# Four buffers instead of two for the selective scan, and two-column-block weight loads for the experts, in a four-layer kernel

## The chip, the cores and the metric

The kernel runs on the 8 cores of one Trainium2 chip. Each core gets one of the 8 sequences of the batch (2048 tokens of 1024 features) and a copy of all weights, and works through the whole four-layer model alone. There is no traffic between cores.
The metric is the device time of the slowest core in microseconds. Engines are named as in the profile: PE is TensorE, DVE is VectorE, ACT is ScalarE, POOL is GpSimd.

## The reference

Each layer is `x = x + s * g`, where `s` is a sequence mixer and `g` a SiLU of a feed-forward part, both taken from the layer-normed `x`. What matters for this change is the selective scan of layer 0 and the experts and the attention of layer 2:

```python
# layer 0, mixer: d_inner = 2048 channels, 16 states, 2048 steps
dA = jnp.exp(dt_i[..., None] * A)
h  = dA * h + dt_i[..., None] * B_i[:, None, :] * x_i[..., None]
y  = jnp.einsum('bds,bs->bd', h, C_i)
...
# layer 2, feed-forward: 8 experts, each takes its k best tokens
k = int(EXPERT_CAPACITY * t / e)
g, m = jax.lax.top_k(probs.transpose(0, 2, 1), k)
h = jax.nn.gelu(jnp.einsum('nekd,edf->nekf', x[batch_idx, m], w1))   # 1024 -> 4096
h = jnp.einsum('nekf,efd->nekd', h, w2)                               # 4096 -> 1024
...
# layer 2, mixer: causal attention, 16 heads of 64, w_qkv and w_out
```

Here `k` is 512 tokens for each expert (2.0 * 2048 / 8).

## The kernel before, in words

Each engine has its own instruction list, written out in Python order, and five engines meet only through semaphores. The helper `emit` makes every instruction of an engine wait for the engine's own previous instruction too, so nothing of one engine overlaps with itself. `barrier` separates the four layers.

**Layer 0.** The 2048 tokens go in 8 slices of 256. In each slice the projections of `W_in`, a convolution, the low-rank feed-forward and the broadcast of B and C come first. Then the scan stage runs over 16 blocks `ct` of 128 channels. A block begins with `dt` (L635, L640, L642), and DVE's `dtx = dt * x` (L646). Then there are 16 steps `s`, one for each state. In each step

- ACT computes `exp(dt * A[s])` into one of two buffers `da2` (L655),
- POOL computes `u = dtx * B[s]` into one of two columns of `m8`, 7 or 6 (L659); an element there stands every 8 elements,
- DVE scans along the 256 tokens with both as inputs and writes column `s` of `Hbuf` (L664).

Because there are two buffers of each kind, ACT and POOL wait in step `s` for the scan of step `s-2`. After the 16 scans DVE alone does the block's end: it saves the last state (L670), multiplies by C (L672), adds the 16 states in a tree (L674 to L681), and applies D and the gate (L683, L687). The tree uses the columns of `m8` that held `u`. Then comes `dtx` of the next block, for which POOL waits.

**Layer 2.** For each of the 8 experts and each half `ic` of its tokens (256), a loop over `fc` goes through 32 blocks of 128 hidden columns. PE computes the hidden block of `fc` (8 matmuls of L270 into `pmisc` or `ptp`), ACT applies the Gelu (L1433), and PE then adds the product of the block `fc-1` with `w2` (8 matmuls, L1447). Weights stream through two buffers each: `w1_ld` fetches 128 columns of `w1`, `w2_ld` 128 rows of `w2`. All these DMAs are issued by POOL in order (L204), and each waits for PE to have used up what stood in its buffer. The attention behind it has a third stream `qkv_ld` with buffers of its own, and `w_out` comes through `w1_ld`.

Of the kernel before, what the change touches and what calls it, by code (L numbers as in the profile page):

```python
# [15 lines left out]
T = 2048  # L16
# [5 lines left out]
TS = 256  # L22
# [96 lines left out]
def build_program(active=(0, 1, 2, 3)):  # L119
# [7 lines left out]
    W = {}  # L127
# [42 lines left out]
    wbuf_t = sbt("wbuf", [128, 10240], BF16)  # L170
    pers_t = sbt("pers", [128, 8704], BF16)
# [27 lines left out]
    STA = F32Arena()  # L199
    WB = ColArena(wbuf_t, 10240)  # L200
# [142 lines left out]
    def make_stream(buf2):  # L343
        sems = (stream_sem_pool.pop(0), stream_sem_pool.pop(0))
        state = {"last": [0, 0]}

        def load(idx, dram_ap, reshape=None, rows=128):
            bufv = buf2[0:rows, idx % 2, :]
            if reshape:
                bufv = bufv.rearrange(reshape[0], **reshape[1])  # L350
            b.wait("gpsimd", "T", state["last"][idx % 2])
            return bufv, (sems[idx % 2],
                          dma("gpsimd", bufv, dram_ap, sems[idx % 2]))

        def consumed(idx, ttarget):
            state["last"][idx % 2] = ttarget
        return load, consumed

    def layer0():
# [60 lines left out]
        m8 = AR.alloc(TS * 8, "p (t s) -> p t s", t=TS)  # L420
# [9 lines left out]
        prod = ybuf[:, 0:8, :]  # L430
        xp_f = STA.alloc(TS)
        dt_f = STA.alloc(TS)
        da2 = [STA.alloc(TS), STA.alloc(TS)]
        cacc2 = [STA.alloc(TS), STA.alloc(TS)]

        b.emit("gpsimd", lambda e: e.memset(hstate[:, :, :], 0.0))
# [12 lines left out]
        for sl in range(NS2):  # L449
# [176 lines left out]
            scan_tgts = []  # L626
            dtx_tgt = 0
            for ct in range(16):
                bi = pbi[0] % POOLN[0]
                pbi[0] += 1  # L630
                bank = pb[bi]
                prev = evac_after_bank.get(bi)
                if prev is not None:
                    b.wait("tensor", prev[0], prev[1])
                b.emit("tensor", lambda e, ct=ct, p=bank: e.matmul(  # L635
                    p[:, 0:TS], wdt[0:64, ct, :], xp_bf[0:64, :],
                    start=True, stop=True), inc="T")
# [12 lines left out]
                for s in range(DS):  # L650
                    if len(scan_tgts) >= 2:
                        b.wait("scalar", "V", scan_tgts[-2])
                        b.wait("gpsimd", "V", scan_tgts[-2])
                    b.emit("scalar", lambda e, ct=ct, s=s, d=da2[s % 2]:
                           e.activation(out=d, in_=dt_f, func=AF.Exp,  # L655
                                        scale=a_sb[:, ct, s:s+1]), inc="S")
                    sS = b.cnt["S"]
                    gU = b.emit("gpsimd", lambda e, s=s, u=ub2[s % 2]:
                                e.tensor_mul(out=u, in0=dtx,  # L659
                                             in1=brep[:, s, :]), inc="G")  # L660
                    b.wait("vector", "S", sS)
                    b.wait("vector", "G", gU)
                    stg = b.emit("vector", lambda e, ct=ct, s=s, d=da2[s % 2],
                                 u=ub2[s % 2]: e.tensor_tensor_scan(  # L664
                                     out=Hbuf[:, :, s], data0=d,
                                     data1=u,
                                     initial=hstate[:, ct, s:s+1],
                                     op0=ALU.mult, op1=ALU.add), inc="V")
# [529 lines left out]
    def layer2():  # L1198
# [23 lines left out]
        cumf = pers_t[:, 4096:8192].bitcast(F32)  # L1222
        PT = pers_t[:, 0:8192].rearrange("p (tt i) -> p tt i", tt=16)
        cmask = pers_t[:, 8192:8320]
        w1_buf = WB.alloc(2 * 1024, "p (b2 m) -> p b2 m", b2=2)
        w2_buf = WB.alloc(2 * 1024, "p (b2 m) -> p b2 m", b2=2)
        XgT = WB.alloc(8 * 512, "p (k i) -> p k i", k=8)
        hT2 = [WB.alloc(256), WB.alloc(256)]
        pmisc2 = [pmisc[:, 0:256], ptp2[0].bitcast(F32)[:, 0:256]]
        gwsb = WB.alloc(1024)  # L1230
        gwT = WB.alloc(8 * 8, "p (k e) -> p k e", k=8)
        w1_ld, w1_done = make_stream(w1_buf)
        w2_ld, w2_done = make_stream(w2_buf)

# [25 lines left out]
            tp_state["evacs"].append(vv)  # L1260

        b.wait("tensor", "V", xnV)
        for tt in range(NTT):
            transpose_tiles([(xn[:, tt, dc*128:(dc+1)*128], xnT_tt[:, dc, :])
                             for dc in range(8)])
# [110 lines left out]
            evac_after_bank[bi] = ("V", tgt)  # L1376
        selV = b.cnt["V"]

        b.wait("vector", "V", selV)
        for ex in range(8):  # L1380
            for tt in range(NTT):
# [21 lines left out]
            for ic in range(2):  # L1403
                hgel = {}
                w2bs = {}
                for fc in range(33):
                    if fc <= 31:
                        w1b, t1 = w1_ld(ex*64 + ic*32 + fc,
                                        W["l2_w1"][ex][:, fc*128:(fc+1)*128]
                                        .rearrange("(k p) m -> p k m", p=128),  # L1410
                                        ("p (k m) -> p k m", dict(k=8)))
                        w2b, t2 = w2_ld(ex*64 + ic*32 + fc,
                                        W["l2_w2"][ex][fc*128:(fc+1)*128, :])
                        w2bs[fc] = (w2b, t2)
# [8 lines left out]
                        def evh(e, p, par=fc % 2):  # L1423
# [4 lines left out]
                                  for kt in range(8)], 128, 256, None,  # L1428
# [5 lines left out]
                                              out=hT2[par],  # L1434
                                              in_=pmisc2[par][0:128, 0:256],
                                              func=AF.Gelu), inc="S")
                        w1_done(ex*64 + ic*32 + fc, b.cnt["T"])
                    fo = fc - 1
                    if 0 <= fo <= 31:
                        b.wait("tensor", "S", hgel[fo])  # L1440
# [67 lines left out]
        for dk in range(8):  # L1508
# [5 lines left out]
        xnT = xn.rearrange("p tt d -> p (tt d)").rearrange(  # L1514
            "p (k t) -> p k t", k=8)
        QK = wbuf_t[:, 0:2048]
        Kb = wbuf_t[:, 6816:8864]
        Vp2 = wbuf_t[:, 2048:3088].rearrange("p (kt w) -> p kt w", kt=16)
        wqkv_buf = wbuf_t[:, 3104:5152].rearrange("p (b2 m) -> p b2 m", b2=2)
        wtp_buf = wbuf_t[:, 5152:5664].rearrange("p (k m) -> p k m", k=8)  # L1520
        stage = wbuf_t[:, 5664:6688]
        at4 = pers_t[:, 8192:8704].rearrange("p (s t) -> p s t", s=4)
        cmask2 = wbuf_t[:, 6688:6816]
        ctxh = P_g.rearrange("p i t -> p (i t)").rearrange(
            "p (tt d) -> p tt d", tt=8)
# [668 lines left out]
```

How the kernel before makes its waits and increments, by code:

```python
    def emit(self, eng, fn, inc=None, n=1):  # L43
        esem = self.ESEM.get(eng)
        chain = esem is not None and inc in (None, esem)
        if chain:
            prev = self.cnt[esem]
            eh = self.semh[esem]
            if prev > 0:
                self.prog[eng].append(
                    lambda e, h=eh, v=prev: e.wait_ge(h, v))
            self.cnt[esem] += 1
            tgt = self.cnt[esem]
            def run(e, fn=fn, h=eh):
                fn(e).then_inc(h, 1)
            self.prog[eng].append(run)
            return tgt
        h = self.semh.get(inc)
        if inc is not None:
            self.cnt[inc] += n
        tgt = self.cnt.get(inc)
        def run(e, fn=fn, h=h, n=n, inc=inc):
            r = fn(e)
            if inc is not None:
                r.then_inc(h, n)
        self.prog[eng].append(run)
        return tgt
# [1 line left out]
    def wait(self, eng, sem, val):  # L71
        if val <= 0:
            return
        h = self.semh[sem]
        self.prog[eng].append(lambda e, h=h, v=val: e.wait_ge(h, v))
# [1 line left out]
    def barrier(self):  # L77
# [2 lines left out]
        h = self.semh["bar"]  # L80
        for eng in ENGS:
            es_ = self.ESEM.get(eng)
            if es_ is not None and self.cnt[es_] > 0:
                eh, ev = self.semh[es_], self.cnt[es_]
                self.prog[eng].append(lambda e, h2=eh, v=ev: e.wait_ge(h2, v))
            self.prog[eng].append(lambda e, h=h: e.sem_inc(h, 1))
            self.prog[eng].append(lambda e, h=h, v=tgt: e.wait_ge(h, v))
```

## Time and profile before

| | |
|---|---|
| time, median of 3 runs | 36100.56 us (36100.11 to 36105.73) |
| profiled execution, its own time | 36104.31 us |
| its span, slowest core (core 0) | 36102.3 us |
| spans of the 8 cores | 36067.7 to 36102.3 us |
| granted TensorE clock | 1.0 on every core |
| busy: PE, DVE, ACT, POOL | 47%, 25%, 18%, 14% |

The profiled execution lies 3.75 us above the median of the runs, and 2.0 us of its time lies outside the span. In a row of the profile the engine comes first or second, then the line of the kernel, the operation, what it writes and reads (by the names of the tensors, so that everything in the large work area is `arena`), the partitions and elements, and how many there are. Shares are of the span. No engine is busy over half of the time, so a share by itself tells little: the layers come one behind the other, and each has its own limit.

### The profile page before, as it was taken

To read this page: it belongs to the slowest core of one execution; us is meant where nothing else is said; L and a number is where in the kernel's file an instruction comes from. 1 tells how busy PE (TensorE), PEld (TensorE's weight loads), DVE (VectorE), ACT (ScalarE), POOL (GpSimd) and SP (SyncE) were. 2 spreads that over 40 slices of the span, in tenths; PEclk is the share of its full clock that TensorE was granted. 3 is DMA by queue.
4 is the path that set the end of the run, shared out by engine and by line. 5 is a ranking of instruction groups with operands and counts; after the bars stand their busy time and mean duration, and the time that the engine had idled before them with its cause. 6 is when DMAs were issued, how large, how long until landed. Compare 5 with 4: busy or idle time off the path is not lost.

```text
span 36102.3 us, 268160 instructions; the slowest of 8 cores (36067.7 to 36102.3 us)
## 1 busy us (share of the span) xinstructions
PE 16788.4 (47%) x51767; PEld 5456.9 (15%) x51816; DVE 9026.3 (25%) x17948; ACT 6637.6 (18%) x10746; POOL 5100.0 (14%) x4680
## 2 busy tenths in 40 slices
PE   2221122211555574666666655666444444444444
PEld 0000000000111121111111122222111111111111
DVE  4446644466212213111111111000100000012222
ACT  1111111111000000000000010111256656630000
POOL 3334433344110000111111000000000000000000
DMA  1111011110331011333333300000000000001112
GB/s 26 19 19 13 6 19 19 19 13 7 39 39 20 13 16 17 41 44 45 42 38 41 36 5 3 3 3 3 1 2 1 1 2 1 1 13 26 27 26 35
DMA packets 1385941, 671.96 MB, mean 19 GB/s; under 512 B 986448, under 2 KB 1254000, under 8 KB 1384544
## 3 DMA queue, kind: packets, MB, share of 16 engines
q0 software_dynamic: 1380256, 637.70, 15.4%
q1 hardware_dynamic: 4288, 17.11, 0.1%
q8 instruction: 697, 11.42, 0.1%
q14 instruction: 700, 5.73, 0.1%
HBM read 1283.30 MB, written 8.39 MB: 36 GB/s over the span
## 4 chain that ended last, share of the span: by engine, by line
PE 41%; issue 25%; DVE 15%; ACT 10%; POOL 5%; DMA 2%; DVEq 1%; ACTq 0%; POOLq 0%; another core or an unknown queue 0%; SPq 0%
PE pb L270 22%; DVE arena L664 6%; POOL arena L659 5%; PE pb L1447 4%; PE ptp L294 4%; ACT L1914 4%; PE pmisc L270 2%; PE ptp L270 2%; ACT arena L1917 2%; ACT stat L1914 2%; PE pb L1484 2%; ACT pers L1630 2%; PE pb L1622 1%; DVE arena L672 1%; PE pb L2071 1%
## 5 line engine op out<-in xcount | busy, mean ns | idle before, releaser
L270 PE MATMUL pb<-arena,wbuf 128*128 128x256 bf16 (+2 forms) x7616 | 3316.8, 436 | 3284.1 <-DVE arena L687 1857.5
L659 POOL TENSOR_TENSOR arena<-arena 128x256 bf16<-128x256 bf16 x2048 | 3268.9, 1596 | 2498.0 <-DVE arena L646 1627.6
L664 DVE TENSOR_TENSOR_SCAN arena<-stat,arena 128x256 bf16<-128x256 f32 x2048 | 3269.9, 1597 | 1146.3 <-POOL arena L659 1033.0
L270 PE MATMUL pb<-wbuf,arena 128*128 128x64 bf16 (+2 forms) x9888 | 2814.8, 285 | 1533.3 <-DVE wbuf L300 35.3
L1928 PE MATMUL pb<-arena 128*128 128x65 bf16 x4096 | 885.5, 216 | 2576.7 <-ACT arena L1917 2116.4
L655 ACT ACTIVATE stat<-stat,pers 128x256 f32<-128x256 f32 x2048 | 1040.4, 508 | 4377.7 <-DVE arena L664 4371.4
L635 PE MATMUL pb<-arena,pers 64*128 64x256 bf16 x128 | 47.1, 368 | 3806.8 <-ACT stat L642 3776.6
L1447 PE MATMUL pb<-wbuf 128*128 128x256 bf16 x4096 | 1515.6, 370 | 614.4 <-PE ptp L270 0.2
L294 PE MATMUL ptp<-cstb,wbuf 128*128 128x128 bf16 (+1 forms) x4480 | 1120.0, 250 | 1296.3 <-PE ptp L294 430.9
L270 PEld LDWEIGHTS pb<-arena,wbuf 128*128 128x128 bf16 (+1 forms) x7616 | 845.5, 111 | 5717.4 <-issue 5717.4
L204 POOL DMA_DIRECT2D wbuf<-L_ffn_w x1024 | 735.1, 722 | 5919.9 <-PE ptp L270 4092.4
L270 PEld LDWEIGHTS pb<-wbuf,arena 128*128 128x128 bf16 x9888 | 1036.8, 105 | 3312.4 <-issue 3312.4
L1914 ACT ACT_TABLE_LOAD x1023 | 1312.5, 1283 | 1217.8 <-PE pb L1908 1142.7
L300 DVE COPY wbuf<-ptp 128x128 bf16<-128x128 bf16 (+1 forms) x4480 | 967.6, 216 | 2006.4 <-PE ptp L294 1883.3
L1630 ACT ACTIVATE pers<-pb 128x128 bf16<-128x128 f32 x2176 | 602.8, 277 | 4031.0 <-PE pb L1622 3961.5
L1917 ACT ACT_TABLE_LOAD x1024 | 1313.8, 1283 | 79.7 <-ACT stat L1914 2.5
L1459 DVE CAST pers<-pb 128x256 bf16<-128x256 f32 x128 | 54.3, 425 | 4280.2 <-PE pb L1447 4268.4
L1939 DVE RECIPROCAL stat<-pb 128x4 f32<-128x4 f32 x64 | 11.7, 182 | 4242.0 <-PE pb L1928 4242.0
L1928 PEld LDWEIGHTS pb<-arena 128*128 128x128 bf16 x4096 | 429.1, 105 | 3363.6 <-issue 3363.6
L270 PE MATMUL pmisc<-wbuf 128*128 128x256 bf16 x2048 | 757.8, 370 | 323.0 <-DVE arena L300 9.1
L270 PE MATMUL ptp<-wbuf 128*128 128x256 bf16 x2048 | 757.8, 370 | 307.2
L204 POOL DMA_DIRECT2D wbuf<-L_ffn_W_v x144 | 75.7, 526 | 5737.9 <-PE pb L270 4743.7
(340 smaller groups left out, 16840.7 us busy)
## 6 DMA issues: line engine op xcount, KB each, us to landing
wbuf<-L_ffn_w POOLq DMA_DIRECT2D x1024, 256.0 KB, 4.7
wbuf<-L_attn_W_in POOLq DMA_DIRECT2D x128, 512.0 KB, 5.9
wbuf<-L_attn_W_out POOLq DMA_DIRECT2D x64, 512.0 KB, 6.8
wbuf<-L_ffn_We POOLq DMA_DIRECT2D x64, 512.0 KB, 5.4
wbuf<-L_ffn_W_k POOLq DMA_DIRECT2D x128, 256.0 KB, 3.9
wbuf<-L_ffn_W_r POOLq DMA_DIRECT2D x128, 256.0 KB, 3.9
wbuf<-L_ffn_W_v POOLq DMA_DIRECT2D x128, 256.0 KB, 3.9
wbuf<-L_ffn_V POOLq DMA_DIRECT2D x256, 64.0 KB, 2.5
```

The lines of the kernel that those rows point to most:

```text
L204: return b.emit(queue, lambda e, o=out_ap, i=in_ap, sk=slow_ok: e.dma_start(out=o, in_=i, allow_slow_non_contiguous=sk), inc=sem, n=16)
L270: r=out_rows, c=out_cols: e.matmul(p[0:r, 0:c], lh, rh, start=st_, stop=sp_),
L294: tT = b.emit("tensor", lambda e, s=s, a=srcp, idn=idn: e.transpose(ptp2[s][:, 0:idn], a, ident[0:idn, 0:idn]), inc="T")
L300: e.tensor_copy(out=d, in_=ptp2[s][:, 0:idn]),
L655: e.activation(out=d, in_=dt_f, func=AF.Exp, scale=a_sb[:, ct, s:s+1]), inc="S")
L659: e.tensor_mul(out=u, in0=dtx, in1=brep[:, s, :]), inc="G")
L664: u=ub2[s % 2]: e.tensor_tensor_scan(out=Hbuf[:, :, s], data0=d, data1=u, initial=hstate[:, ct, s:s+1], op0=ALU.mult, op1=ALU.add), inc="V")
L1447: coff=coff, w2b=w2b, par=fo % 2: e.matmul(bank[:, coff:coff+256], w2b[:, mt*128:(mt+1)*128], hT2[par], start=(fo == 0 and mt % 2 == 0), s ...
L1630: p=sbank: e.activation(out=at4[:, sl4, :], in_=p[:, 0:128], func=AF.Exp, scale=0.125),
L1914: e.activation(out=sd2[par], in_=p[:, 0:512], func=AF.Sqrt, bias=1e-12))
L1917: e.activation(out=ksq_at[:, par*512:par*512+512], in_=sd2[par % 2], func=AF.Exp, scale=-1.0), inc="S")
L1928: par=kav % 4, p=cbank: e.matmul(p[:, qm*65:qm*65+65], ksq_at[:, par*512+qm*128: par*512+(qm+1)*128], Vp3[:, kav, :], start=(kav == 0 and ...
```

## The change

There are four edits.

1. In the scan of layer 0 there are four buffers for `exp(dt * A)` and four columns of `m8` (7, 6, 5, 4) for `u`. ACT and POOL wait in step `s` for the scan of step `s-4`.
2. In the experts of layer 2, `w1` is fetched 256 columns at a time, for two values of `fc`, into two buffers of double size. To make room, the Gelu's output moves to `pers`, and the gate's weights lie in the first expert buffers. The first loads of `w1` and `w2` therefore wait for what reads the gate's weights.
3. The attention of layer 2 places its tiles elsewhere in `wbuf`, over memory of the experts that is free by then.
4. `w_out` and `w_qkv` of layer 2 both come through the stream of `w2`. `w_qkv` had its own before.

```diff
-        da2 = [STA.alloc(TS), STA.alloc(TS)]
+        da2 = [STA.alloc(TS), STA.alloc(TS), STA.alloc(TS), STA.alloc(TS)]
...
-                ub2 = [m8[:, :, 7], m8[:, :, 6]]
+                ub4 = [m8[:, :, 7], m8[:, :, 6], m8[:, :, 5], m8[:, :, 4]]
                 b.wait("gpsimd", "V", dtx_tgt)
                 for s in range(DS):
-                    if len(scan_tgts) >= 2:
-                        b.wait("scalar", "V", scan_tgts[-2])
-                        b.wait("gpsimd", "V", scan_tgts[-2])
+                    if len(scan_tgts) >= 4:
+                        b.wait("scalar", "V", scan_tgts[-4])
+                        b.wait("gpsimd", "V", scan_tgts[-4])
...
-        w1_buf = WB.alloc(2 * 1024, "p (b2 m) -> p b2 m", b2=2)
+        w1_buf = WB.alloc(2 * 2048, "p (b2 m) -> p b2 m", b2=2)
...
-        hT2 = [WB.alloc(256), WB.alloc(256)]
+        hT2 = [pers_t[:, 8192:8448], pers_t[:, 8448:8704]]
...
-        gwsb = WB.alloc(1024)
-        gwT = WB.alloc(8 * 8, "p (k e) -> p k e", k=8)
+        gwsb = w1_buf[:, 0, 0:1024]
+        gwT = w2_buf[:, 0, 0:64].rearrange("p (k e) -> p k e", k=8)
...
+        w1_done(0, b.cnt["T"]); w1_done(1, b.cnt["T"])
+        w2_done(0, b.cnt["T"]); w2_done(1, b.cnt["T"])
...
                     if fc <= 31:
-                        w1b, t1 = w1_ld(ex*64 + ic*32 + fc,
-                                        W["l2_w1"][ex][:, fc*128:(fc+1)*128]
+                        if fc % 2 == 0:
+                            w1b2, t1 = w1_ld(ex*32 + ic*16 + fc//2,
+                                             W["l2_w1"][ex][:, fc*128:(fc+2)*128]
...
+                        w1b = w1b2[:, :, (fc % 2)*128:(fc % 2)*128+128]
+                        t1 = t1_hold
...
-                        w1_done(ex*64 + ic*32 + fc, b.cnt["T"])
+                        if fc % 2 == 1:
+                            w1_done(ex*32 + ic*16 + fc//2, b.cnt["T"])
...
-        Kb = wbuf_t[:, 6816:8864]
-        Vp2 = wbuf_t[:, 2048:3088].rearrange("p (kt w) -> p kt w", kt=16)
-        wqkv_buf = wbuf_t[:, 3104:5152].rearrange("p (b2 m) -> p b2 m", b2=2)
+        Kb = wbuf_t[:, 2048:4096]
+        Vp2 = wbuf_t[:, 6144:7184].rearrange("p (kt w) -> p kt w", kt=16)
...
-        qkv_ld, qkv_done = make_stream(wqkv_buf)
+        qkv_ld, qkv_done = w2_ld, w2_done
...
-            wob, t3 = w1_ld(512 + rb, W["l2_wout"][rb*128:(rb+1)*128, :])
+            wob, t3 = w2_ld(512 + rb, W["l2_wout"][rb*128:(rb+1)*128, :])
...
-            w1_done(512 + rb, b.cnt["T"])
+            w2_done(512 + rb, b.cnt["T"])
```

In the scan stage no instruction moves, only what it waits for. On POOL, in the first slice of layer 0, from the last small DMA before the scan stage to the loads of `W_out` behind it (V, G and T are the semaphores of DVE, POOL itself and PE):

```order
 L204 DMA arena<-arena 1x16x256 [waits T]
 L659 TENSOR_TENSOR arena<-arena 128x256 [waits V,G]
-L659 TENSOR_TENSOR arena<-arena 128x256 [waits G]
-L659 TENSOR_TENSOR arena<-arena 128x256 [waits V,G] x254
+L659 TENSOR_TENSOR arena<-arena 128x256 [waits G] x3
+L659 TENSOR_TENSOR arena<-arena 128x256 [waits V,G] x252
 L204 DMA wbuf<-L_attn_W_out 128x16x128 x2
 L204 DMA wbuf<-L_attn_W_out 128x16x128 [waits T] x6
```

The multiplications stand where they stood; the first four of them, instead of the first two, wait for no scan, and the later ones wait for an older scan.

On POOL at the start of the experts of layer 2, the DMA issues before the change:

```order
L204 DMA wbuf<-L2_ffn_gate_w 8x1024
L204 DMA wbuf<-L2_ffn_w1 128x8x128
L204 DMA wbuf<-L2_ffn_w2 128x1024
L204 DMA wbuf<-L2_ffn_w1 128x8x128
L204 DMA wbuf<-L2_ffn_w2 128x1024
L204 DMA wbuf<-L2_ffn_w1 128x8x128 [waits T]
L204 DMA wbuf<-L2_ffn_w2 128x1024 [waits T]
```

and the same place in the changed kernel:

```order
L204 DMA wbuf<-L2_ffn_gate_w 8x1024
L204 DMA wbuf<-L2_ffn_w1 128x8x256 [waits T]
L204 DMA wbuf<-L2_ffn_w2 128x1024 [waits T] x2
L204 DMA wbuf<-L2_ffn_w1 128x8x256 [waits T]
L204 DMA wbuf<-L2_ffn_w2 128x1024 [waits T] x2
L204 DMA wbuf<-L2_ffn_w1 128x8x256 [waits T]
```

One load of `w1` now comes for every two of `w2`, it is twice as wide, and the first loads wait for PE as well.

## Rows read from the trace of the kernel before

**Rows 1.** Busy time by stage: layer 0, layer 1, experts, attention, layer 3.
```profile
core 0: us, PE busy (x) PEld busy (x) DVE busy (x) ACT busy (x) POOL busy (x), PEclk, DMA share, GB/s
0.00:9060.00 9060.00, 1821.41 (x4976) 526.02 (x4976) 4978.15 (x4418) 1531.85 (x3076) 3790.09 (x2781) 1.00 0.14 16
...
14220.00:20390.00 6170.00, 4269.69 (x10692) 1126.55 (x10736) 671.44 (x1575) 197.38 (x513) 733.29 (x1022) 1.00 0.39 44
```

**Rows 2.** Groups by line, layer 0's scan: busy, mean ns | idle before, releaser.
```profile
L659 POOL TENSOR_TENSOR arena<-arena 128x256 bf16<-128x256 bf16 x2048 | 3268.9, 1596 | 2498.0 <-DVE arena L646 1627.6
L664 DVE TENSOR_TENSOR_SCAN arena<-stat,arena 128x256 bf16<-128x256 f32 x2048 | 3269.9, 1597 | 1146.3 <-POOL arena L659 1033.0
...
L655 ACT ACTIVATE stat<-stat,pers 128x256 f32<-128x256 f32 x2048 | 1040.4, 508 | 4377.7 <-DVE arena L664 4371.4
```

**Rows 3.** Timeline of DVE, first block's end to the second's begin.
```profile
613.02 1.30 DVE L664 TENSOR_TENSOR_SCAN arena<-stat,arena 128x256 bf16<-128x256 f32 x1 [0.46 <-DVE arena L664]
...
623.50 0.42 DVE L646 TENSOR_TENSOR arena<-stat,arena 128x256 bf16<-128x256 f32 x1
...
667.55 0.42 DVE L646 TENSOR_TENSOR arena<-stat,arena 128x256 bf16<-128x256 f32 x1
```

**Rows 4.** Timeline, first steps of the block at 623.50: start us, us.
```profile
624.19 1.32 POOL L659 TENSOR_TENSOR arena<-arena 128x256 bf16<-128x256 bf16 x1 [12.21 <-DVE arena L646]
...
625.66 1.35 POOL L659 TENSOR_TENSOR arena<-arena 128x256 bf16<-128x256 bf16 x1
625.69 1.90 DVE L664 TENSOR_TENSOR_SCAN arena<-stat,arena 128x256 bf16<-128x256 f32 x1 [1.76 <-POOL arena L659]
...
627.69 1.32 DVE L664 TENSOR_TENSOR_SCAN arena<-stat,arena 128x256 bf16<-128x256 f32 x1
...
627.79 1.94 POOL L659 TENSOR_TENSOR arena<-arena 128x256 bf16<-128x256 bf16 x1 [0.78 <-DVE arena L664]
...
629.87 1.33 POOL L659 TENSOR_TENSOR arena<-arena 128x256 bf16<-128x256 bf16 x1
```

**Rows 5.** Timeline, three pairs with another distance between the two starts.
```profile
545.57 1.34 POOL L659 TENSOR_TENSOR arena<-arena 128x256 bf16<-128x256 bf16 x1
545.95 1.54 DVE L664 TENSOR_TENSOR_SCAN arena<-stat,arena 128x256 bf16<-128x256 f32 x1 [1.24 <-POOL arena L659]
...
675.94 1.31 DVE L664 TENSOR_TENSOR_SCAN arena<-stat,arena 128x256 bf16<-128x256 f32 x1
...
676.33 1.64 POOL L659 TENSOR_TENSOR arena<-arena 128x256 bf16<-128x256 bf16 x1 [1.08 <-DVE arena L664]
...
1632.43 1.30 DVE L664 TENSOR_TENSOR_SCAN arena<-stat,arena 128x256 bf16<-128x256 f32 x1 [0.89 <-POOL arena L659]
1632.69 1.77 POOL L659 TENSOR_TENSOR arena<-arena 128x256 bf16<-128x256 bf16 x1 [0.43 <-POOL arena L659]
```

**Rows 6.** Groups by line, stage of the experts.
```profile
L270 PE MATMUL pmisc<-wbuf 128*128 128x256 bf16 x2048 | 757.8, 370 | 323.0 <-DVE arena L300 9.1 <-DVE arena L1500 7.8 <-DVE arena L1494 1.1
```

**Rows 7.** Timeline of one loop turn in the experts, PE and POOL.
```profile
15580.33 0.37 PE L270 MATMUL ptp<-wbuf 128*128 128x256 bf16 x1
15580.73 1.43 POOL L204 DMA_DIRECT2D wbuf<-L_ffn_w  x2 [6.88 <-PE ptp L270]
...
15588.65 0.37 PE L270 MATMUL pmisc<-wbuf 128*128 128x256 bf16 x1
```

**Rows 8.** DMA issues: KB each, median us from issue to landing.
```profile
wbuf<-L_attn_W_in POOLq DMA_DIRECT2D x128, 512.0 KB, 5.9
...
wbuf<-L_attn_Wq_l POOLq DMA_DIRECT2D x64, 256.0 KB, 4.6
```

**Rows 9.** Landing of one pair of loads, of `w2` and `w1`, issued at 15514.2.
```profile
DMA to landing us min/median/max: 4.0/4.8/5.6
```

**Rows 10.** Timeline of POOL, last load of `w_out`, first of `w_qkv`.
```profile
20572.87 0.54 POOL L204 DMA_DIRECT2D wbuf<-L_attn_w_out  x1 [3.17 <-PE ptp L294]
20573.40 1.07 POOL L204 DMA_DIRECT2D wbuf<-L_attn_w_qkv  x2
```

More of the change, by code:

```diff
@@ L647, in layer0 @@
                     out=dtx, in0=dt_f, in1=xi[:, ct, 3:3+TS]), inc="V")
-                ub2 = [m8[:, :, 7], m8[:, :, 6]]
+                ub4 = [m8[:, :, 7], m8[:, :, 6], m8[:, :, 5], m8[:, :, 4]]
                 b.wait("gpsimd", "V", dtx_tgt)
                 for s in range(DS):
-                    if len(scan_tgts) >= 2:
-                        b.wait("scalar", "V", scan_tgts[-2])
-                        b.wait("gpsimd", "V", scan_tgts[-2])
-                    b.emit("scalar", lambda e, ct=ct, s=s, d=da2[s % 2]:
+                    if len(scan_tgts) >= 4:
+                        b.wait("scalar", "V", scan_tgts[-4])
+                        b.wait("gpsimd", "V", scan_tgts[-4])
+                    b.emit("scalar", lambda e, ct=ct, s=s, d=da2[s % 4]:
                            e.activation(out=d, in_=dt_f, func=AF.Exp,
@@ L657, in layer0 @@
                     sS = b.cnt["S"]
-                    gU = b.emit("gpsimd", lambda e, s=s, u=ub2[s % 2]:
+                    gU = b.emit("gpsimd", lambda e, s=s, u=ub4[s % 4]:
                                 e.tensor_mul(out=u, in0=dtx,
@@ L662, in layer0 @@
                     b.wait("vector", "G", gU)
-                    stg = b.emit("vector", lambda e, ct=ct, s=s, d=da2[s % 2],
-                                 u=ub2[s % 2]: e.tensor_tensor_scan(
+                    stg = b.emit("vector", lambda e, ct=ct, s=s, d=da2[s % 4],
+                                 u=ub4[s % 4]: e.tensor_tensor_scan(
                                      out=Hbuf[:, :, s], data0=d,
@@ L1262, in layer2 @@
         b.wait("tensor", "V", xnV)
+        gw_guard = [False]
         for tt in range(NTT):
@@ L1407, in layer2 @@
                     if fc <= 31:
-                        w1b, t1 = w1_ld(ex*64 + ic*32 + fc,
-                                        W["l2_w1"][ex][:, fc*128:(fc+1)*128]
-                                        .rearrange("(k p) m -> p k m", p=128),
-                                        ("p (k m) -> p k m", dict(k=8)))
+                        if fc % 2 == 0:
+                            w1b2, t1 = w1_ld(ex*32 + ic*16 + fc//2,
+                                             W["l2_w1"][ex][:, fc*128:(fc+2)*128]
+                                             .rearrange("(k p) m -> p k m",
+                                                        p=128),
+                                             ("p (k m) -> p k m", dict(k=8)))
+                            t1_hold = t1
+                        w1b = w1b2[:, :, (fc % 2)*128:(fc % 2)*128+128]
+                        t1 = t1_hold
                         w2b, t2 = w2_ld(ex*64 + ic*32 + fc,
@@ L1516, in layer2 @@
         QK = wbuf_t[:, 0:2048]
-        Kb = wbuf_t[:, 6816:8864]
-        Vp2 = wbuf_t[:, 2048:3088].rearrange("p (kt w) -> p kt w", kt=16)
-        wqkv_buf = wbuf_t[:, 3104:5152].rearrange("p (b2 m) -> p b2 m", b2=2)
-        wtp_buf = wbuf_t[:, 5152:5664].rearrange("p (k m) -> p k m", k=8)
-        stage = wbuf_t[:, 5664:6688]
+        Kb = wbuf_t[:, 2048:4096]
+        Vp2 = wbuf_t[:, 6144:7184].rearrange("p (kt w) -> p kt w", kt=16)
+        wtp_buf = wbuf_t[:, 8208:8720].rearrange("p (k m) -> p k m", k=8)
+        stage = wbuf_t[:, 7184:8208]
         at4 = pers_t[:, 8192:8704].rearrange("p (s t) -> p s t", s=4)
-        cmask2 = wbuf_t[:, 6688:6816]
+        cmask2 = wbuf_t[:, 8720:8848]
         ctxh = P_g.rearrange("p i t -> p (i t)").rearrange(
             "p (tt d) -> p tt d", tt=8)
-        qkv_ld, qkv_done = make_stream(wqkv_buf)
+        qkv_ld, qkv_done = w2_ld, w2_done
         b.wait("vector", "S", g2S)
@@ L1553, in layer2 @@
         b.wait("vector", "D1", b.cnt["D1"])
-        sidx = [0]
+        b.wait("vector", "D2", b.cnt["D2"])
+        b.wait("vector", "D3", b.cnt["D3"])
+        sidx = [1000]
         def proj_rows(dram_rowblk, dst_row, src0, ncols):
```

## The prediction

> **What bounds the kernel now.** I first read the busy time by stage, because no engine is busy over half of the whole. The four layers share the time one after the other, and the change touches two stages. Layer 0 is 9060 us, in which DVE is busy for 4978 us and POOL for 3790 us; the experts of layer 2 are 6170 us, in which PE is busy for 4270 us [rows 1].
>
> In layer 0 the groups by line show a loop of three engines. 2048 multiplications on POOL and 2048 scans on DVE take 1596 and 1597 ns in the mean, ACT's exponentials only 508 ns; POOL and DVE both stand idle for part of the loop, and ACT's long idle time ends with a scan, so ACT isn't the limit [rows 2]. The timeline of DVE gives the length of a block of 16 steps: from one `dtx` to the next, 667.55 - 623.50 = 44.05 us [rows 3]. There are 8 slices of 16, so 128 blocks, or about 5640 us. A block has two parts. Its end runs on DVE alone, from the last scan's end at 613.02 + 1.30 = 614.32 to POOL's first multiplication at 624.19, 9.87 us [rows 3, 4]. The other 34.2 us are the 16 steps, and two steps repeat every 629.87 - 625.66 = 4.21 us [rows 4].
>
> Why 2.10 us for a step, when either instruction alone takes 1.3? The single instructions show it. Alone, a multiplication takes 1.32 to 1.35 us. A scan that starts 0.03 us after a multiplication takes 1.90; a multiplication that starts 0.10 us after a scan takes 1.94, and the scan then takes 1.32 [rows 4]. So whoever starts second is held up by about 0.6 us. Three rarer pairs tell how [rows 4, 5]:
>
> - scan 0.03 us later: it ends at 627.59, the multiplication at 627.01, so 0.58 us apart; scan 0.38 us later: 547.49 against 546.91, 0.58 again
> - multiplication 0.10 us later: 629.73 against 629.01, 0.72 apart; 0.26 later: 1634.46 against 1633.73, 0.73; 0.39 later: 677.97 against 677.25, 0.72
>
> The distance of the ends doesn't depend on how long the two overlapped. This is not a sharing of speed. It is a part at the end that each can do only when the other is through: 0.72 us of a multiplication and 0.58 us of a scan. The rest (1.335 - 0.72 = 0.61 and 1.31 - 0.58 = 0.73) goes on freely beside the other.
>
> With two buffers the loop now reads: a scan ends, 0.20 us later the multiplication that waited for its buffer starts (627.59 to 627.79), takes 1.94, the next one follows 0.14 later and takes 1.33, and its neighbour, the scan that started 0.03 after it, ends 0.58 behind it. That is 0.20 + 1.94 + 0.14 + 1.33 + 0.58 = 4.19, as measured. The wait for the buffer is what puts one multiplication of two behind a scan, into the held state.
>
> **The change part by part.** *Scan, four buffers.* Nothing is added or removed, only the wait is for step `s-4`. POOL is then free to run one multiplication after the other, 1.335 + 0.145 (from 625.51 to 625.66) = 1.48 us for a step [rows 4]. Does the scan hold it up? A scan whose free part is done when a multiplication ends needs 0.58 us more. The next multiplication starts 0.145 us after that end and needs nothing exclusive for its first 0.61 us, so until 0.755 after it. The scan is through by 0.58. Exclusive parts add up to 1.30 us for a step, under 1.48. So POOL sets the pace, and DVE (scan of 1.31 to 1.38 and 0.10 between two) follows it. POOL never gets more than two steps ahead; ACT at 508 ns for a step has room, and four buffers suffice.
>
> A block then is: 16 x 1.335 + 15 x 0.145 = 23.5 us of multiplications; the scan before the last ends 0.58 after, the last one 0.10 + 1.31 later, together 25.5; and the end of 9.87 as before, since POOL waits for the next `dtx` as it did. That is 35.4 against 44.05, so 8.65 to 8.7 us for a block, and x128 = 1110 us. Bounds: at best no exclusive part bites at all, and the last scan ends 0.16 + 1.31 behind the last multiplication, 0.5 us a block or 70 us more gain. At worst each step is a full multiplication and a full scan one behind the other (rival D below), a loss. I take the first, to which all five pairs lie near. The cover that ends goes nowhere else: behind the scans POOL issues `W_out`'s loads as early before the block's end as now, as its last multiplication stays about 2 us ahead of the last scan's end.
>
> At this place the Trainium skill has a rule. "SBUF — State Buffer", section "Who interferes with whom", says that a DVE instruction with two SBUF inputs takes the read interface that GpSimd reads through, that who issues first has it for the whole instruction and that the other blocks fully. The trace agrees that the second waits for the first's end. It disagrees on the price: a fully blocked multiplication would end 1.3 us behind the scan, and it ends 0.72 behind it. What the rule would make of the new loop is rival D.
>
> *Experts, w1 in pairs.* PE's turn takes 15588.65 - 15580.33 = 8.32 us, 16 x 0.52, and PE's idle time before the first group is 323.0 us over 2048 matmuls, 0.16 us, the same as between any two [rows 6, 7]. No weight is late now, so half as many loads gain nothing: 0. Can they lose? The pair for the turns 2i and 2i+1 stands on POOL behind `w2` of turn 2i-1, so it is issued at the same place as now, one turn ahead: `w1` goes out 0.55 us after 15580.73 and is needed at 15588.6, 7.3 us later [rows 7]. A load of this very shape, `W_in`'s, lands after 5.9 us; one of the old shape after 4.6, or 5.6 behind a `w2` [rows 8, 9]. So I expect 5.9 + 1.0 = 6.9 us, just under 7.3, and cost 0. If it came no later than now (5.6) nothing would change; if it had to wait for `w2` to land (4.0), 9.9 us, PE would stand 2.6 us for each of 256 pairs, 670 us. I keep that end for the range.
>
> *The rest.* The first loads of the experts wait for the router's transposes, but before they are used PE does 128 gather matmuls, not under 0.37 us each, 47 us. `w_qkv`'s first two loads, which now follow `w_out`'s last at once [rows 10], will wait for two groups of transposes; at most one landing of 4.6 us shows, once. Moved tiles change no instruction's shape. Together 0 to 5 us.
>
> The sum, against the profiled execution: 36104.3 - 1110 = 34994. That execution lies 3.75 us above the runs' median, so 34990.
>
> **The rivals.** *A, sharing of speed.* The second instruction runs at half speed while both run. The pair 0.10 apart fits (1.22 us together, 0.6 lost). Then a step has 2.645 us of work, done at 1.53 while both run and at 1 in the two gaps of 0.245: 0.245 + 2.40/1.53 = 1.81 us. A block would be 1.5 + 16 x 1.81 - 0.1 + 9.87 = 40.2, the gain 490 us, the time 35610. Against it: 0.92 us together should cost 0.46, and cost 0.31 [rows 5].
>
> *B, start in a held part.* In all pairs the second started within 0.39 us of the first. In the new loop multiplications start while a scan is in its exclusive part. If it can do nothing there, it ends 0.58 + 1.335 = 1.92 after the one before: the gain is 2.07 us a block, 265 us, 35840. Against it: in the pair 0.39 apart the scan's exclusive part began 0.34 after the multiplication's start, and that one had done its 0.61 all the same.
>
> *C, no gain.* Every instruction that starts beside another pays the 0.6 in full. POOL's step is 1.93 + 0.145 = 2.08, a block 44.4, and the time stays at 36100.
>
> *D, slower.* Four buffers let both engines always be ready, and the loop falls into strict turns: 1.335 + 1.31 = 2.65 us a step, a block 1.3 + 42.4 + 9.87 = 53.6, 9.55 x 128 = 1220 us more, 37320. It is slower from the point where a step exceeds 2.10. For it speaks only that so steady an overlap isn't in the trace; against it the 0.61 and 0.73 that every pair does for free. It is what the rule of the Trainium skill gives ("SBUF — State Buffer", as above).
>
> *E, w1 late.* The gain of the scan less up to 670: 35660.
>
> **How the numbers follow.** The forecast has 0.68, A 0.10, B 0.06, C 0.06, D 0.06, E 0.04. The range starts at 34900, under the best case of 34920, and goes to 35700 over A and E; B, C and D, 0.18, are left out. The forecast's own range is 34900 to 35080. Faster by over 0.2% (72 us, about what a measurement of this kernel tells from no change): 0.88; within it 0.06; slower 0.06.
>
> **What would show it.** Multiplications of 1.34 and scans near 1.38 us in the mean, with hardly any of 1.9; POOL's steps 1.48 us apart; blocks of 35.4 us; layer 0 ending near 7950 us. Busy time of both engines falls to about 2750 and 2800 us. In the experts turns stay at 8.32 us, and PE has no idle time that ends with a landing of `w1`. I am wrong if scans or multiplications keep a second group at 1.9 us, or if PE's turns grow beyond 8.4 us on every second `fc`.

## The result and the profile after

The changed kernel takes 35033.9 us (median of 8 runs, 35026.7 to 35048.0), the kernel before 36102.7 us beside it (8 runs, 36100.1 to 36110.8). The ratio is 0.9704 (95% interval 0.9693 to 0.9714): 3% faster, 1069 us. The prediction was 34990 us, in a range of 34900 to 35700.

The groups by line of the changed kernel, in the same columns as [rows 2, 6]:

```profile
L664 DVE TENSOR_TENSOR_SCAN arena<-stat,arena 128x256 bf16<-128x256 f32 x2048 | 2886.0, 1409 | 433.3 <-POOL arena L659 227.2
L659 POOL TENSOR_TENSOR arena<-arena 128x256 bf16<-128x256 bf16 x2048 | 2748.9, 1342 | 1921.5 <-DVE arena L646 1641.5
...
L270 PE MATMUL pmisc<-wbuf 128*128 128x256 bf16 x2048 | 759.9, 371 | 349.1 <-DMA wbuf<-L_ffn_w 33.0
```

The mean multiplication fell from 1596 to 1342 ns and the mean scan from 1597 to 1409, though neither instruction was touched. In the experts PE now waits 33.0 us in all for the `w1` loads. On the other cores it is 27.9 to 44.9 us; before, no core waited for them at all.

The block of 16 steps, as in [rows 3], and the first steps of one, as in [rows 4], from the changed kernel's timeline (start us, us):

```profile
1465.95 0.42 DVE L646 TENSOR_TENSOR arena<-stat,arena 128x256 bf16<-128x256 f32 x1
1492.35 0.17 DVE L670 COPY arena<-arena 128x16 bf16<-128x16 bf16 x1
1501.43 0.43 DVE L646 TENSOR_TENSOR arena<-stat,arena 128x256 bf16<-128x256 f32 x1
...
1502.12 1.32 POOL L659 TENSOR_TENSOR arena<-arena 128x256 bf16<-128x256 bf16 x1 [11.87 <-DVE arena L646]
1503.62 1.90 DVE L664 TENSOR_TENSOR_SCAN arena<-stat,arena 128x256 bf16<-128x256 f32 x1 [1.76 <-POOL arena L659]
...
1508.03 1.34 POOL L659 TENSOR_TENSOR arena<-arena 128x256 bf16<-128x256 bf16 x1
1508.58 1.39 DVE L664 TENSOR_TENSOR_SCAN arena<-stat,arena 128x256 bf16<-128x256 f32 x1
1509.51 1.34 POOL L659 TENSOR_TENSOR arena<-arena 128x256 bf16<-128x256 bf16 x1
1510.07 1.37 DVE L664 TENSOR_TENSOR_SCAN arena<-stat,arena 128x256 bf16<-128x256 f32 x1
```

A block takes 1501.43 - 1465.95 = 35.48 us instead of 44.05, so 8.57 x 128 = 1097 us are won in the scan stage. The first scan of a block is still held (1.90 us): that is so in 126 of the 128 blocks. From then on POOL runs one multiplication every 1509.51 - 1508.03 = 1.48 us at its bare 1.34 us (15 of the 2048 take 1.47), and each scan ends about 0.60 us behind the multiplication beside it (1509.97 against 1509.37). This is the loop of the prediction.

The loads, as in [rows 8], each with its median time from issue to landing; first `w1` (the 512 KB loads), then `w2`:

```profile
wbuf<-L_ffn_w POOLq DMA_DIRECT2D x256, 512.0 KB, 6.3
wbuf<-L_ffn_w POOLq DMA_DIRECT2D x512, 256.0 KB, 3.9
```

And the wait that is new, in the list of who waited for whom in the experts (us in total, times, longest). Some 0.15 us of each of the 33 lie between any two groups of matmuls anyway, so about 33.0 - 33 x 0.15 = 28 us are new:

```profile
PE pmisc L270 <- DMA wbuf<-L_ffn_w: 33.0, 33, 2.1
```

### The profile page after: what moved, and what is told of

Read it like the earlier page. It is cut to its first block, busy times and chain, and to the rows that moved or that the text cites. A ratio compares the mean times of both kernels' runs of the same rounds, so it can differ in the third digit from the quotient of the medians.

```text
span 35033.7 us, 267673 instructions; the slowest of 8 cores (34982.7 to 35033.7 us)
## 1 busy us (share of the span) xinstructions
PE 16838.4 (48%) x51816; PEld 5451.5 (16%) x51816; DVE 8645.5 (25%) x17948; ACT 6654.0 (19%) x10746; POOL 4346.5 (12%) x4424
## 4 chain that ended last, share of the span: by engine, by line
PE 42%; issue 25%; DVE 18%; ACT 11%; DMA 3%; DVEq 1%; POOL 1%; ACTq 0%; POOLq 0%; SPq 0%
PE pb L270 22%; DVE arena L664 8%; PE ptp L294 4%; PE pb L1456 4%; ACT L1924 4%; PE pmisc L270 2%; PE ptp L270 2%; ACT arena L1927 2%; ACT stat L1924 2%; PE pb L1493 2%; ACT pers L1640 2%; PE pb L1632 1%; DVE arena L672 1%; PE pb L2081 1%; PE pb L1693 1%
## 5 line engine op out<-in xcount | busy, mean ns | idle before, releaser
L664 DVE TENSOR_TENSOR_SCAN arena<-stat,arena 128x256 bf16<-128x256 f32 x2048 | 2886.0, 1409 | 433.3 <-POOL arena L659 227.2
L659 POOL TENSOR_TENSOR arena<-arena 128x256 bf16<-128x256 bf16 x2048 | 2748.9, 1342 | 1921.5 <-DVE arena L646 1641.5
L1456 PE MATMUL pb<-pers,wbuf 128*128 128x256 bf16 x4096 | 1519.6, 371 | 610.3 <-PE ptp L270 0.2
L204 POOL DMA_DIRECT2D wbuf<-L_ffn_w x768 | 501.6, 656 | 6182.0 <-PE pmisc L270 3533.0
L1441 ACT ACTIVATE pers<-pmisc 128x256 bf16<-128x256 f32 x256 | 98.6, 385 | 4020.6 <-PE pmisc L270 4020.6
```

The lines of the kernel that those rows point to most:

```text
L659: e.tensor_mul(out=u, in0=dtx, in1=brep[:, s, :]), inc="G")
L664: u=ub4[s % 4]: e.tensor_tensor_scan(out=Hbuf[:, :, s], data0=d, data1=u, initial=hstate[:, ct, s:s+1], op0=ALU.mult, op1=ALU.add), inc="V")
L1456: coff=coff, w2b=w2b, par=fo % 2: e.matmul(bank[:, coff:coff+256], w2b[:, mt*128:(mt+1)*128], hT2[par], start=(fo == 0 and mt % 2 == 0), s ...
```

## The experiments

Each was measured beside the kernel before, which took 36098.4 us beside the first four, 36098.3 beside the next four and 36096.8 beside the last two. Ratios are to these. Beside the changed kernel it took 36102.7 us, so a difference from the changed kernel, taken from the times as they stand, can be off by some 4 to 6 us.

### Edit 1 alone, and the rest alone

The kernel before with edit 1, the four scan buffers:

> The kernel before with the four scan buffers alone. Theory: the whole gain is the scan stage's (8 slices, 5649 to 4552 us in the two traces) and the double w1 load is a small loss, so this is faster than the changed kernel by the 28 us that PE's turns in the experts have grown: 36103 - 1097 = 35006 us. Rival (the merged weight streams or the half as many DMAs of the experts bring part of the gain): later than the changed kernel, above 35034.

Measured: 35005.7 us (35001.7 to 35008.4), ratio 0.9698 (0.9683 to 0.9712). The converse is the changed kernel with edit 1 taken back:

```diff
-        da2 = [STA.alloc(TS), STA.alloc(TS), STA.alloc(TS), STA.alloc(TS)]
+        da2 = [STA.alloc(TS), STA.alloc(TS)]
...
-                    if len(scan_tgts) >= 4:
+                    if len(scan_tgts) >= 2:
...
```

> The changed kernel with the two scan buffers of before, so the w1 loads in pairs and the moved tiles alone. Theory: PE waits for a w1 pair that lands more than 7.3 us after its issue, in all some 28 us: 36103 + 28 = 36131 us. Rival (fewer descriptors relieve the DMA engines and POOL and that pays): 36103 or less. Rival of the prediction's upper end (w1 must wait for w2 to land): 36103 + 670.

Measured: 36127.3 us (36112.6 to 36137.4, and one of the ten runs at 36277.7), ratio 1.0012 (1.0003 to 1.0022). So edit 1 brings the whole gain and more, and the rest of the change costs 24 to 29 us: 35033.9 - 35005.7 = 28.2, or 24 when each is taken against the kernel before beside it, and 36127.3 - 36098.4 = 28.9. Both theories that gave the experts' edits a gain fall, and so does the price of 670 us.

The traces say where the cost lies. The stretch from the choice of the experts' tokens (its last scan, L1351 of the changed kernel) to the issue of the last `w_out` load, which holds the experts, takes 6511 us in the median of the cores before and with edit 1 alone, and 6539 us in the changed kernel.

### The w1 pairs one turn earlier

```diff
+                def ld_pair(pr, ex=ex, ic=ic, w1pf=w1pf):
+                    w1pf[pr] = w1_ld(ex*32 + ic*16 + pr, ...)
+                ld_pair(0)
                 for fc in range(33):
                     if fc <= 31:
                         if fc % 2 == 0:
-                            w1b2, t1 = w1_ld(ex*32 + ic*16 + fc//2, ...
+                            w1b2, t1_hold = w1pf.pop(fc//2)
+                        elif fc < 31:
+                            ld_pair(fc//2 + 1)
                         ...
                         w2b, t2 = w2_ld(...)
```

> The changed kernel, but POOL issues each w1 pair one turn earlier, ahead of the w2 load of the odd turn. Theory: with 15 us instead of 7.3 between issue and use no landing (longest 9.2 us) is late, PE's turns are 8.32 us everywhere and the time is 35034 - 28 = 35006. Rival (the 28 us come from something else in the new layout, as the Gelu's output in another tensor or slower PE turns): stays at 35034.

Measured: 34995.2 us (34993.7 to 35015.7), ratio 0.9696 (0.9682 to 0.9711). That is 39 us under the changed kernel, not 28. The stretch with the experts is back at 6511 us, so 28 of them are the loads'. The rest hangs on the slowest core, whose time the metric is: by the median of the eight cores' spans this run is 29 us faster (35011 to 34982). It also lies under edit 1 alone, by 10 us, or by 6 in the median of the cores (34988). That difference is in the stretch ahead of the experts, from the end of layer 0's scans on (5001 us against 5010), and it has come up in layer 1 already, in which edits 2 to 4 change no instruction. Its cause isn't known. The waits are gone; PE's first group in the experts now reads

```profile
L270 PE MATMUL pmisc<-wbuf 128*128 128x256 bf16 x2008 | 745.0, 371 | 314.0 <-DVE arena L300 7.9 <-DVE arena L1514 7.8 <-DVE arena L1508 1.1
```

with no DMA among the releasers. Landings as late as 9.0 us are still there. The loads only have twice the time.

```profile
DMA to landing us min/median/max: 3.7/5.2/9.0
```

### Three buffers

```diff
-                    if len(scan_tgts) >= 4:
-                        b.wait("scalar", "V", scan_tgts[-4])
+                    if len(scan_tgts) >= 3:
+                        b.wait("scalar", "V", scan_tgts[-3])
...
-                    b.emit("scalar", lambda e, ct=ct, s=s, d=da2[s % 4]:
+                    b.emit("scalar", lambda e, ct=ct, s=s, d=da2[(ct*DS + s) % 3]:
...
```

> The changed kernel with three scan buffers instead of four. Theory of the held part: POOL is never more than two steps ahead of the finished scan, so the third buffer is all that is needed, blocks stay at 35.5 us and the time at 35034. Rival (buffers work as slack against jitter, each one more brings a part): a block between 44.1 and 35.5, about 38 to 40, time 35350 to 35600.

Measured: 35030.4 us (35023.4 to 35035.5), ratio 0.9704 (0.969 to 0.9719), with scans of 1381 ns in the median as with four. The fourth buffer brings nothing that these runs show, so buffers don't act as slack here; what counts is that a multiplication need not wait for the scan that has just ended.

### One input of the scan in PSUM

This is the test of where the exclusive part comes from. The scan reads `exp(dt * A)` and `u`, both in SBUF. Here ACT writes the first to banks of PSUM that are free at that time; with two buffers, on the kernel before:

```diff
-        da2 = [STA.alloc(TS), STA.alloc(TS)]
+        da2 = [pmisc[:, 0:TS], pb[4][:, 0:TS]]
```

> The kernel before (two buffers), but ACT writes exp(dt * A) into two banks of PSUM, so the scan has one input in SBUF instead of two. Theory R (the held part is the read interface that DVE and GpSimd share, and only a scan with two SBUF inputs needs it): nothing is held, scans take 1.31 to 1.35 and multiplications 1.34 us at any distance of the starts, two steps take 0.20 + 1.34 + 0.16 + 1.31 = 3.0 instead of 4.2 us, a block about 35.5, and the time falls to about 35000 with two buffers and no other change. Theory W (the held part is the strided writing of both): pairs, blocks and time stay as before, 36100 (with scans 0.05 us longer or shorter by the other source).

Measured: 35004.2 us (34998.6 to 35010.2), ratio 0.9698 (0.9683 to 0.9712). That is as much as edit 1 gains, with two buffers and nothing else changed; that the two gains come out equal is chance, since here the wait for the buffer sets the pace (3.0 us for two steps) and there POOL does. All 2048 multiplications fall into one narrow group, and so do the scans of either bank:

```profile
L664 DVE TENSOR_TENSOR_SCAN arena<-pmisc,arena x1024: 1299/1316/1335, 445.3 to 7952.0; 128x256 bf16<-128x256 f32 x171
L664 DVE TENSOR_TENSOR_SCAN arena<-pb,arena x1024: 1287/1317/1335, 446.8 to 7953.5; 128x256 bf16<-128x256 f32 x171
...
L659 POOL TENSOR_TENSOR arena<-arena x2048: 1319/1342/1359, 443.8 to 7952.0; 128x256 bf16<-128x256 bf16 x187
```

(min/median/max ns). And in the timeline a multiplication and a scan that start 0.03 or 0.04 us apart leave each other alone, where [rows 4] has 1.90 us for a scan 0.03 and 1.94 us for a multiplication 0.10 us behind the other:

```profile
1512.69 1.35 POOL L659 TENSOR_TENSOR arena<-arena 128x256 bf16<-128x256 bf16 x1
1512.72 1.32 DVE L664 TENSOR_TENSOR_SCAN arena<-pmisc,arena 128x256 bf16<-128x256 f32 x1 [1.76 <-POOL arena L659]
...
1514.21 1.32 DVE L664 TENSOR_TENSOR_SCAN arena<-pb,arena 128x256 bf16<-128x256 f32 x1 [0.17 <-DVE arena L664]
1514.25 1.34 POOL L659 TENSOR_TENSOR arena<-arena 128x256 bf16<-128x256 bf16 x1 [0.21 <-DVE arena L664]
```

The edit also takes ACT's writing out of SBUF, but that isn't what held the other two. In the kernel before, the scan at 625.69 of [rows 4] is held to 1.90 us, and ACT's next instruction comes only after it, behind 12.77 us of idle time:

```profile
627.74 0.51 ACT L655 ACTIVATE stat<-stat,pers 128x256 f32<-128x256 f32 x1 [12.77 <-DVE arena L664]
```

With four buffers, on the changed kernel (banks `pmisc`, `pb[4]` and the two of the transposes):

> The changed kernel (four buffers) with exp(dt * A) in four banks of PSUM. Theory R: the second group of scans at 1.38 us goes, no scan is held, POOL still sets the pace with 1.48 us a step, and a block ends 0.5 us earlier: 35034 - 70 = 34965 us. Theory W: 35034.

Measured: 34960.2 us (34955.0 to 34967.2), ratio 0.9686 (0.9671 to 0.97), 74 us under the changed kernel (69 when each is taken against the kernel before beside it), near the 70 us that the prediction gave as its best case. The theory that the strided writing excludes the other falls in both. The exclusive part exists only while the scan takes two inputs from SBUF. Here the trace agrees with the Trainium skill ("SBUF — State Buffer", section "Who interferes with whom"), which gives a second SBUF input of a DVE instruction the read interface that GpSimd uses.

### u in contiguous rows

```diff
-                ub4 = [m8[:, :, 7], m8[:, :, 6], m8[:, :, 5], m8[:, :, 4]]
+                ub4 = [xn[:, 0, j*TS:(j+1)*TS] for j in range(4)]
```

> The changed kernel, but POOL writes u into four contiguous rows of a buffer that is free at that time, instead of every eighth element of m8. Theory W (writing with a stride is what makes the last 0.72 us of a multiplication, and it is what excludes the scan): the multiplication falls to 0.6 to 0.7 us, nothing is held, DVE sets the pace with 1.31 + 0.10, a block is about 33.2 us and the time 34740. Theory R with a price of the stride on top: the multiplication is shorter but the reading still excludes, so late scans are still held (scans above 1.35 us), a block between 33.5 and 35. Rival (1.33 us is POOL's time for 256 elements, whatever the stride): 35034.

Measured: 34779.1 us (34774.6 to 34779.6), ratio 0.9635 (0.9621 to 0.9649). The stride costs half of a multiplication, and yet instructions are still held. The time near 34740 was right and the theory beside it (W, nothing is held) wrong; what came is theory R with a price of the stride, with a block of 33.51 us at the lower end of its 33.5 to 35.

```profile
1512.57 0.67 POOL L659 TENSOR_TENSOR arena<-arena 128x256 bf16<-128x256 bf16 x1
1512.60 1.73 DVE L664 TENSOR_TENSOR_SCAN arena<-stat,arena 128x256 bf16<-128x256 f32 x1 [1.10 <-POOL arena L659]
1513.38 1.02 POOL L659 TENSOR_TENSOR arena<-arena 128x256 bf16<-128x256 bf16 x1
1514.43 1.30 DVE L664 TENSOR_TENSOR_SCAN arena<-stat,arena 128x256 bf16<-128x256 f32 x1
...
1514.54 1.25 POOL L659 TENSOR_TENSOR arena<-arena 128x256 bf16<-128x256 bf16 x1
```

The first multiplication needs 0.67 us. The scan beside it ends at 1514.33, which is 1.09 us behind the multiplication's end, not 0.58. The next two multiplications end 0.07 and 0.06 us behind their scan (1514.40 against 1514.33, 1515.79 against 1515.73), not 0.72. DVE now sets the pace: 1.30 + 0.10 us a step. The scan reads `u` contiguously here and still takes 1.30 us, so the stride of this input costs it nothing.

### State-by-state layout

`H`, `C` and `m8` are stored with the 256 tokens of one state side by side; the instructions stay the same.

```diff
-        Hbuf = AR.alloc(TS * 16, "p (t s) -> p t s", t=TS)
+        Hbuf = AR.alloc(16 * TS, "p (s t) -> p s t", s=16)
...
-                                     out=Hbuf[:, :, s], data0=d,
+                                     out=Hbuf[:, s, :], data0=d,
...
-                ub4 = [m8[:, :, 7], m8[:, :, 6], m8[:, :, 5], m8[:, :, 4]]
+                ub4 = [m8[:, 7, :], m8[:, 6, :], m8[:, 5, :], m8[:, 4, :]]
...
```

> The changed kernel with H, C and m8 stored state by state instead of token by token, so that scans, multiplications and the additions behind them all read and write contiguous rows; the same instructions. Theory (the stride costs half or more of each 256-element instruction, as 0.42 us for dtx against 1.30 for an addition in m8 lets one guess): scan about 0.6, steps 0.8 us, the end of a block about 8 instead of 9.9, a block near 21 us, the time about 33200. Rival (the scan's 1.31 us is its recurrence, 5 ns an element): DVE paces at 1.41, a block about 31, the time about 34450. Rival (no effect of strides): 35034.

Measured: 33513.6 us (33508.3 to 33519.1), ratio 0.9284 (0.9269 to 0.93). The scan's own 1.31 us was its stride too, that of its output after what the run above showed of `u`: alone it now takes 0.75 us (the minimum below), held 0.90.

```profile
L664 DVE TENSOR_TENSOR_SCAN arena<-stat,arena x2048: 749/904/1186, 427.9 to 6441.9; 128x256 bf16<-128x256 f32 x187
...
L659 POOL TENSOR_TENSOR arena<-arena x2048: 662/865/1081, 427.1 to 6440.4; 128x256 bf16<-128x256 bf16 x187
```

A step is 1.0 us rather than the 0.8 expected, and a block 24.5 rather than 21. Unheld, a step would be 0.75 + 0.10 = 0.85, so 0.05 of the miss is the scan's own time (0.6 expected) and the rest is that the two hold each other again, which the theory had forgotten:

```profile
1507.95 0.86 POOL L659 TENSOR_TENSOR arena<-arena 128x256 bf16<-128x256 bf16 x1
1508.46 0.90 DVE L664 TENSOR_TENSOR_SCAN arena<-stat,arena 128x256 bf16<-128x256 f32 x1
1508.96 0.87 POOL L659 TENSOR_TENSOR arena<-arena 128x256 bf16<-128x256 bf16 x1
```

The scan ends 0.55 us behind the first multiplication (1509.36 against 1508.81), and the second multiplication 0.47 behind the scan (0.46 in the median). Added up they are the step: 1.01 us.

### All together, with four and with two buffers

> State-by-state layout, exp(dt * A) in four banks of PSUM, four buffers, and w1 pairs issued one turn early, all together. With the layout alone a block took 24.7 us, with steps of 1.0 us (scan 0.905 held, 0.75 alone, gap 0.10). Theory R: nothing is held any more, DVE sets the pace with 0.75 + 0.10 = 0.85 us, a block is 16 x 0.15 = 2.5 us shorter, 320 us in all, and 28 to 39 us more by the earlier w1: 33514 - 350 = 33160 us. Rival (the reading of contiguous rows is short and hardly held): only the w1 part, 33480.

Measured: 33159.0 us (33151.5 to 33168.8), ratio 0.9186 (0.9171 to 0.9202). Scans and multiplications are at their bare length everywhere, and nothing is held:

```profile
L665 DVE TENSOR_TENSOR_SCAN arena<-ptp,arena x1024: 749/750/752, 436.2 to 6116.2; 128x256 bf16<-128x256 f32 x171
...
L660 POOL TENSOR_TENSOR arena<-arena x2048: 661/667/672, 433.7 to 6114.7; 128x256 bf16<-128x256 bf16 x187
```

> The same as the kernel above with two scan buffers instead of four: what edit 1 is worth once nothing is held. Theory (what four buffers bring is that they take the multiplication out from behind the scan it waited for; without an exclusive part there is little to bring): two steps take 0.20 + 0.67 + 0.16 + 0.75 = 1.78 against 2 x 0.85 = 1.70, a block 0.6 us longer, 33160 + 80 = 33240 us. Rival (the number of buffers matters by itself, at 2.1 to 1.48 us a step as before): 33160 + 500 or more.

Measured: 33243.3 us (33240.4 to 33259.5), ratio 0.921 (0.9197 to 0.9224). The buffers of edit 1 are now worth 84 us instead of about 1097. With four buffers, the version with all of it beats both kernels, by 8% the one before and by 5% the changed one.

## Why the prediction was right, and where it was off

**The mechanism.** Its central step, that the multiplication and the scan hold each other by a fixed part and that four buffers take the multiplications out from behind the scan, stands. The step came at 1.48 to 1.49 us against 1.48, the block at 35.48 against 35.4, the stage's gain at 1097 us against 1110. Three buffers do the same. Taking the collision away does as much with two, and once it is gone four buffers bring 84 us: so it is the held part, not the number of buffers, that made edit 1 worth 1097. Scans of 1.9 us are left only at the start of a block (126 of 2048). "Hardly any of 1.9" in the prediction's signs was too strict, and they bring the mean scan to 1409 ns and DVE's busy time to 2886 us instead of 1380 and 2800. They cost no pace, since POOL runs on beside them.

**The rivals.** Sharing of speed (A) gave a block of 40.2 us and held starts (B) a gain of 2.07 us, so 42.0; neither is there. (A's sum divides by 1.53 where half speed gives 1.5; done rightly its block is 40.8 and its time 35680, still inside the range.) C would have left scans or multiplications at 1.9 us all along a block, and D would have spread the steps to 2.65 us. The rule of the Trainium skill ("SBUF — State Buffer", "Who interferes with whom") was right on what collides. Read as a block over the whole recorded duration it would have given a loss, D, and the trace after shows none.

**Where in the instruction the exclusive part lies was misread.** The prediction put it at the end: 0.58 us of a scan, 0.72 of a multiplication. With a short multiplication the scan behind it needs 1.09 us after the multiplication's end, and a multiplication behind a scan only 0.07. Suppose that a contiguous multiplication reads until its end. Then a scan needs about 1.09 us from the moment it may read, having done only 1.31 - 1.09 = 0.22 before, and a multiplication whose writing is strided is through with reading about 1.09 - 0.58 = 0.51 us ahead of its end. What excludes is the reading, early in a strided instruction; the rest of the strided writing comes after it and hinders nobody. The layout run tests this. With both contiguous, each has again done 0.2 us before it is held (0.75 - 0.55 of a scan, 0.67 - 0.46 of a multiplication). A strided scan then lets the other go 0.46 - 0.07 = 0.39 us ahead of its end, and a strided multiplication behind it should end 1.335 - 0.21 - 0.39 = 0.73 us after it; [rows 4, 5] have 0.72. So this reading fits the pairs of all these kernels and the PSUM runs, but where the reading begins and ends was not measured by itself. It left the sum right because only the sum of the exclusive parts (1.30 us a step, the same in either reading) had to stay under POOL's 1.48.

**The term that was mis-sized** is `w1` in pairs: 0 predicted, 33.0 us of waits in the trace, which is 28 beyond the usual gaps, and 24 to 29 us by the two experiments. The step that failed was to set a median against a fixed limit. 6.9 us expected and 6.3 measured in the median are under 7.3, but a load's landing varies (in the loop up to 8.3 us on this core; the 9.2 of the first loads is hidden), and so does the limit. In 20 of the pairs POOL stood 0.85 us between `w2` and `w1`, and nothing in the profile says for what, so only 6.4 us were left:

```profile
15579.58 0.53 POOL L204 DMA_DIRECT2D wbuf<-L_ffn_w  x1 [7.78 <-PE ptp L270]
15580.96 0.89 POOL L204 DMA_DIRECT2D wbuf<-L_ffn_w  x1 [0.85 <-issue]
15589.49 0.37 PE L270 MATMUL pmisc<-wbuf 128*128 128x256 bf16 x1 [2.13 <-DMA wbuf<-L_ffn_w]
```

Nineteen of the 33 waits, with 22.4 of the 33.0 us, follow such a pause, and the longest is this one. The kernel before has such pauses ahead of its expert loads too (43, 25.7 us in all), but its `w1` lands earlier. The sum with that term, 34990 + 13 + 28 = 35031, is near the measured 35034; the 13 are the scan stage's, 1110 less 1097. That it is this near is partly luck: the waits differ by 17 us between the cores.

**The rest.** The first expert loads, the merged streams of `w_out` and `w_qkv` and the moved tiles were put at 0 to 5 us. With the early loads the stretch with the experts takes what it takes with edit 1 alone (6511 us), and the one behind it, to the last `w_qkv` load, 4540 us in both, so these edits cost nothing that shows. The prediction's "layer 0, 9060 us" ends just behind the last scan (9053.7); the last product with `W_out` comes after it, which changes none of its sums.

## What to carry to other kernels

When two engines' instructions have two lengths in the trace, set the end of the later one against the end of the earlier one for several distances of their starts. A difference that stays constant is exclusion. If it grows as much as the distance, the two leave each other alone, and if it grows by a part of it, they share speed. Exclusion and sharing give other gains for the same edit. Then ask whether the collision can be removed (one operand in PSUM) before making room for it with buffers, and look at the stride of 256-element instructions first of all: here the layout was worth 1520 us, the buffers 1097 and PSUM 1094. A load whose median landing is just in time is still late whenever it lands slowly or is issued late, so count on the slowest cases.

## What was not expected of the hardware

- A bf16 row of 256 written with a stride of 8 elements costs POOL 1.34 us for a multiplication, and 0.67 us contiguous. The scan written with a stride of 16 elements takes 1.31 us, and 0.75 contiguous, so its recurrence wasn't its limit at 1.31.
- On DVE, the last addition of the tree (L681) fell from 1.30 to 0.29 us, the one with D (L683) from 1.35 to 0.48 and the gate (L687) from 0.60 to 0.29, with the layout alone. The large multiplication by C (L672), contiguous in both, stayed at 2.29.
- A scan with its first input in PSUM is no slower than with both in SBUF (0.750 us in the contiguous layout, 1.32 in the strided).

In the changed layout, from its groups by line:

```profile
L672 DVE TENSOR_TENSOR arena<-arena 128x4096 bf16<-128x4096 bf16 x128 | 293.4, 2292 | 13.7 <-DVE arena L670 0.5
...
L683 DVE SCALAR_TENSOR_TENSOR arena<-arena,pers 128x256 bf16<-128x256 bf16 x128 | 61.9, 484 | 14.2 <-DVE arena L681 1.4
...
L687 DVE TENSOR_TENSOR arena<-arena 128x256 bf16<-128x256 bf16 x128 | 37.4, 292 | 13.4
L681 DVE TENSOR_TENSOR arena<-arena 128x256 bf16<-128x256 bf16 x128 | 37.4, 292 | 13.7 <-DVE arena L679 0.5
```

and in the changed kernel L681 (min/median/max ns) and, from its timeline, one L683 and one L687:

```profile
L681 DVE TENSOR_TENSOR arena<-arena x128: 1295/1296/1298, 468.0 to 7951.8; 128x256 bf16<-128x256 bf16 x128
```

```profile
1499.27 1.35 DVE L683 SCALAR_TENSOR_TENSOR arena<-arena,pers 128x256 bf16<-128x256 bf16 x1
1500.73 0.60 DVE L687 TENSOR_TENSOR arena<-arena 128x256 bf16<-128x256 bf16 x1
```
